# Moving four things forward in a three-phase mixture-of-experts kernel's instruction streams: the last phase's first table, the next phases' row loads, the first half's inverse roots and two scatters

## The reference, cut to what matters

```python
x = x + 0.5 * ffn(layernorm(x))      # 12 experts, each token goes to 3 of them
x = x + attn(layernorm(x))           # gates, y_t = A*y_{t-1} + u_t along 512 tokens, norm, gated product
x = x + 0.5 * ffn(layernorm(x))
# ffn: top-3 of x @ Wg (128x12), softmax weights, h = gelu(x @ Wup[e] + bup[e]) (128 -> 512),
#      y = h @ Wdown[e] + bdown[e] (512 -> 128), sum over the 3 chosen experts
```

## Time and profile before

| what | value |
|---|---|
| median of 3 runs | 632.81 us (632.74 to 634.7) |
| profiled execution | 633.43 us, its span in the trace 631.7 us |
| TensorE matmul busy | 564.4 us (89% of the span) |
| ScalarE busy | 419.8 us (66%) |
| GpSimd busy | 418.0 us (66%) |
| VectorE busy | 348.7 us (55%) |
| mean granted TensorE clock | 0.954 of full speed |

### The profile page before, as it was taken

How to read it: one execution, slowest core, us unless ns; L and a number is a source line. 1 busy time by engine, 2 the same in 40 slices (tenths; PEclk the granted TensorE clock), 3 DMA queues, 4 the chain that set the end, 5 groups by cost and what they waited for, 6 DMA issues and landing times.

```text
span 631.7 us, 17884 instructions
## 1 busy us (share of the span) xinstructions
PE 564.4 (89%) x4591; PEld 529.5 (84%) x4591; DVE 348.7 (55%) x1636; ACT 419.8 (66%) x1280; POOL 418.0 (66%) x432
## 2 busy tenths in 40 slices
PE   8469999999699999999999899999979999989505
PEld 7358999999699889879899789899979999989502
DVE  5983365371014688987727589888743532232206
ACT  2547686686366787887668688877657766656204
POOL 1137777777767775556677777066666777777774
PEclk9769999999799999999999999999999999999957
DMA  7577776789598786466478967466568888765137
GB/s 214 180 190 236 211 196 202 218 205 275 156 288 255 215 240 178 138 188 189 135 215 255 275 212 206 148 187 183 160 175 249 217 281 251 215 194 156 49 119 244
DMA packets 121847, 127.90 MB, mean 202 GB/s; under 512 B 17178, under 2 KB 84561, under 8 KB 121749
## 3 DMA queue, kind: packets, MB, share of 16 engines
q1 hardware_dynamic: 106452, 99.52, 53.2%
q0 software_dynamic: 12992, 26.11, 14.8%
q10 hardware_dynamic: 2304, 1.11, 0.6%
HBM read 96.62 MB, written 30.79 MB: 202 GB/s over the span
## 4 chain that ended last, share of the span: by engine, by line
PE 54%; DMA 13%; POOL 12%; DVE 10%; issue 8%; ACT 1%; SPq 0%; DVEq 0%; POOLq 0%; ACTq 0%
PE ps L931 20%; PE ps L944 20%; POOL YG L739 6%; DMA YG<-ys,SY 4%; POOL yk L750 3%; PE ps L799 3%; DMA xl<-xn,SG 3%; PE ps L825 2%; POOL xs L723 2%; PE ps L901 2%; DMA yk<-Ys,row 2%; DMA xs<-XN,SX 2%; PE ps L891 1%; DMA ys<-Ys 1%; DVE YG L1563 1%
## 5 line engine op out<-in xcount | busy, mean ns | idle before, releaser
L1097 ACT ACTIVATE hT<-ps,BU 128x128 f32<-128x128 f32 x944 | 269.4, 371 | 109.3 <-PE ps L931 106.7
L931 PE MATMUL ps<-xT,WU 128*128 128x128 f32 x1888 | 253.8, 278 | 4.2 <-ACT hT L1097 2.3
L944 PE MATMUL ps<-WD,hT 128*128 x1888 | 252.4, 277 | 4.8 <-DVE Ys L1635 3.7
L931 PEld LDWEIGHTS ps<-xT,WU 128*128 128x128 f32 x1888 | 233.4, 194 | 13.9 <-issue 13.9
L944 PEld LDWEIGHTS ps<-WD,hT 128*128 128x128 f32 x1888 | 231.7, 193 | 6.9 <-issue 6.8
L723 POOL DMA_INDIRECT xs<-XN,SX x144 | 144.5, 1004 | 87.6 <-issue 66.2
L739 POOL DMA_INDIRECT YG<-ys,SY x144 | 150.1, 1042 | 48.5 <-issue 40.6
L1635 DVE TENSOR_TENSOR Ys<-ps,BD 128x128 f32<-128x128 f32 x236 | 67.5, 289 | 193.4 <-PE ps L944 182.7
L708 POOL DMA_INDIRECT xl<-xn,SG x59 | 59.7, 1011 | 30.4 <-issue 14.0
L750 POOL DMA_INDIRECT yk<-Ys,row x59 | 59.0, 1000 | 18.0 <-issue 13.2
L1074 ACT ACTIVATE xT<-ps 128x512 f32<-128x512 f32 (+1 forms) x55 | 32.6, 593 | 6.6 <-PE ps L901 2.9
(11 more groups left out here) (255 smaller groups left out, 540.1 us busy)
## 6 DMA issues: line engine op xcount, KB each, us to landing
WU<-in_L_ffn_Wup_dram SPq DMA_DIRECT2D x236, 256.0 KB
ys<-Ys SPq DMA_DIRECT2D x42, 256.0 KB
xl<-xs SPq DMA_DIRECT2D x118, 66.0 KB, 3.0
xl<-xs SPq DMA_DIRECT2D x59, 64.0 KB, 1.9
WD<-in_L_ffn_Wdown_dram SPq DMA_DIRECT2D x12, 256.0 KB, 4.9
WD<-yk SPq DMA_DIRECT2D x4, 768.0 KB, 7.2
xs<-XN,SX POOLq DMA_INDIRECT x144
YG<-ys,SY POOLq DMA_INDIRECT x144
```

Source lines behind the costliest of these rows:

```text
L931: x = e.matmul(HB[i % 2][:, c * P:(c + 1) * P], WU[i % NW][:, c * P:(c + 1) * P], xT[m % 2][:, j * P:(j + 1) * P], start=True, stop=True)
L944: x = e.matmul(YB[i % 2][:, 0:D], hT[i % 3][:, c * P:(c + 1) * P], WDf[:, bass.ds(r + c * P, P)], start=(c == 0), stop=(c == C - 1))
L1097: x = e.activation(hT[i % 3][:, c * P:(c + 1) * P], HB[i % 2][:, c * P:(c + 1) * P], ACT.Gelu, bias=BU[:, bass.ds(b + c, 1)])
```

## The change

Four moves, with no arithmetic added or removed:

1. VectorE's steps A0, A1, A2 for phase 3 go from slots 51, 52, 53 to slots 49, 50, 51.
2. FETCHED is 0 for k = 0 and 1, so phase 3's scatters 0 and 1 stand ahead of all gathers. From scatter 2 on the order is as before.
3. SP's `load_rows` for the next phase's groups 0 and 1 move from behind tiles 56 and 57 to behind tiles 55 and 56, in phases 0, 1 and 2. SP's weight load of tile 56 is thereby behind the first of them, and that of tile 57 behind both.
4. In `first()`, all four `stats`, the 16 aggregations (in two groups of 8) and the root's first steps are placed between the four `chosen`. Three steps and everything else of the root's tail stay behind the one-hot arrays.

```diff
-TABLES_AT = ((34, 38), (50, 63), (51, 64))
-FETCHED = tuple(min(K * NT, 6 + (13 * k) // 25) for k in range(NTL))
+TABLES_AT = ((34, 38), (50, 63), (49, 64))
+FETCHED = tuple(min(K * NT, 6 + (13 * k) // 25) if k > 1 else 0 for k in range(NTL))
...
-                if n + 1 < NPH and k in (NTL - 3, NTL - 2):
-                    load_rows(NG * (n + 1) + k - (NTL - 3))
+                if n + 1 < NPH and k in (NTL - 4, NTL - 3):
+                    load_rows(NG * (n + 1) + k - (NTL - 4))
...
+                def spread(a, b):
+                    e.wait_ge(s_dv, dv.n)
+                    for t in range(a, b):
+                        i = e.bn_aggr(mv16[:, t, :], st16[:, t, :])
+                    dv.on(i)
+                    e.wait_ge(s_dv, dv.n)
...
-                for q in range(NQ):
-                    chosen(q)
-                    if q + 2 < NQ:
-                        stats(q + 2)
+                stats(2)
+                chosen(0)
+                stats(3)
+                spread(0, NT // 2)
+                chosen(1)
+                spread(NT // 2, NT)
+                dv.on(e.tensor_scalar(v16[:], mv16[:, :, 1], 1e-5, None, ALU.add))
+                e.wait_ge(s_dv, dv.n)
+                dv.on(e.tensor_scalar(nr16[:].bitcast(I32), v16[:].bitcast(I32), -0.5, RSQRT_SEED, ALU.mult, ALU.add))
+                e.wait_ge(s_dv, dv.n)
+                dv.on(e.tensor_tensor(na16[:], v16[:], nr16[:], ALU.mult))
+                e.wait_ge(s_dv, dv.n)
+                chosen(2)
+                dv.on(e.tensor_tensor(nb16[:], na16[:], nr16[:], ALU.mult))
+                e.wait_ge(s_dv, dv.n)
+                dv.on(e.scalar_tensor_tensor(nb16[:], nb16[:], R1, nb16[:], ALU.add, ALU.mult))
+                e.wait_ge(s_dv, dv.n)
+                dv.on(e.scalar_tensor_tensor(na16[:], nb16[:], R0, na16[:], ALU.add, ALU.mult))
+                dv.on(e.scalar_tensor_tensor(nr16[:], nb16[:], R0, nr16[:], ALU.add, ALU.mult))
+                e.wait_ge(s_dv, dv.n)
+                chosen(3)
...
-                for t in range(NT):
-                    i = e.bn_aggr(mv16[:, t, :], st16[:, t, :])
-                dv.on(i)
...
```

## The result

| | median | runs | ratio to before, 95% interval |
|---|---|---|---|
| before | 634.70 us (632.74 to 636.22) | 9 | |
| after | 628.62 us (626.4 to 631.2) | 9 | 0.9903 (0.9881 to 0.9924) |

The change is faster by 6.2 us where 6.2 us were forecast; the interval allows 4.8 to 7.5, so that the two agree to a tenth is luck. The profiled execution of after took 631.2 us (span 629.5 us) and is the slowest of its nine, against 633.43 us of before: this pair shows 2.2 us. So I read from it the steps, and the sum from the medians.

The account below looks back on a forecast made before the run. Path: VectorE to SG, POOL in phase 0, TensorE and VectorE in phases 1 and 2, POOL in phase 3. 2.98 + 1.6 + 1.58 gives 6.2 us: 627.3 from the profiled 633.43, median forecast 626.7 us, range 625.2 to 629.4.

Parts of the forecast that it names:

- Part 4, 1.58 us: Start of kernel: L1526 waits for TensorE's counts, starts near 21.03 not 22.61, so SG and POOL's stream come 1.58 us earlier.
- The upper bound of 2.5 us: Start of kernel: the most part 4 could gain, if TensorE's counts started sooner.
- Part 1, 1.6 us: End of phase 2: VectorE's K starts 1.6 us earlier, and so do POOL's last 12 scatters.
- Part 2, 2.98 us: Boundary 2/3: two scatters fill POOL's 3.28 us idle, leaving the usual 0.30, so 2.98 us gained.
- Part 3, nothing: Phase boundaries: earlier row loads gain nothing at 0/1 and 1/2, and add nothing to the sum.
- The held weight load: Boundaries: tile 56's weight load waits behind the rows, costed at nothing; as the slower rival about 635 us, chance 0.04.
- The signs that missed: Boundary 2/3: row load near 463.9, 12 scatters near 462.1, L750 rows near 477.6; POOL without a hole to about 618.5.
- Those by which a term vanishes: K not earlier or the start's gain lost: 628.3 us, chance 0.15; only the two scatters count: 630.2 us, 0.06.
- the rival by which it is more: End of phase 2: L not late or K 2.6 us earlier, 7.2 us gained, 625.6 us, chance 0.12.
- the first, third and fourth rival: K not earlier or start's gain lost, 628.3 us, 0.15; more than forecast, 625.6, 0.12; VectorE stops POOL's descriptors, 628.9, 0.03.
- the second's: Boundary 2/3: only the two scatters count, 2.6 us gained, 630.2 us, chance 0.06.
- The one by which VectorE stops POOL's descriptors: End of phase 2: A1 and A2, 2.3 us, are added to POOL's path, gain 3.9 us, 628.9 us, chance 0.03.

Follow-up runs that it names:

- roots: Only part 4 added to the kernel before: 632.46 us, ratio 0.9972.
- no_rows: The whole change without part 3, row loads left as in the kernel before: 627.04 us, ratio 0.9884.
- again: The changed kernel unaltered, run and profiled a second time: 628.01 us beside 634.07 for the kernel before, ratio 0.9893.
- fillers6: The whole change without part 3, with 6 instead of 20 fillers ahead of the counts: 628.42 us, ratio 0.9887.
- rows_b: Only part 3 added to the kernel before, repeated on another chip: 633.94 us beside 635.64, ratio 0.9973.
- rows_02_b: The whole change, but row loads moved only at boundaries 0/1 and 2/3, repeated: 628.14 us, ratio 0.9896.
- rows: Only part 3 added to the kernel before, in the slow job: 954.36 us beside 955.65, ratio 0.9967.

## Why the forecast was right, and where it was not

- **Part 4, 1.58 us.** Right: SG 1.63 us earlier, first gather 1.7 us earlier over ten profiles, 1.8 us by time (0.4 to 3.0). L1534 started at 20.97 where 21.0 was said, and SG at 36.79 where near 37.0 was said. The reason given for the bound is wrong, though: not only the fillers keep the counts from starting sooner, VectorE's own scan does too. The upper bound of 2.5 us could not have been reached by removing them. And the term was carried through phase 0 by the reading that POOL has no hole there, which is wrong: 1.31 us stand at 150.26 us before. The gain passes all the same: the stretch is 124.5 to 126.5 us with part 4 and 124.9 to 126.7 without.
- **Part 1, 1.6 us.** Right in its mechanism, a little small. From the start of the last quarter's residual add (L1312) to POOL's first scatter, the four profiles without part 1 need 13.64 to 13.67 us and the six with it 11.84 to 11.86: 1.8 us. K starts 9.99 us after L1312 (11.79 before). I had let the row maxima start 0.5 us later than before. They start 6.98 us after L1312, and 6.69 before, so 0.3. That this passes to the end by itself is argued from the chain, as part 1 alone has no usable time. VectorE before, then after, with K in the earlier trace rows before:

```profile
451.68 0.69 DVE L1312 TENSOR_TENSOR X<-X,ps 128x512 f32<-128x512 f32 x1 [1.02 <-PE ps L891]
```

```profile
453.84 0.69 DVE L1312 TENSOR_TENSOR X<-X,ps 128x512 f32<-128x512 f32 x1 [0.79 <-PE ps L891]
...
457.68 0.45 DVE L1428 TENSOR_TENSOR ge<-iotl,enda 128x288 f32<-128x288 f32 x1
...
460.03 0.16 DVE L1363 TENSOR_SCALAR eR<-RR 1x24 uint32<-1x24 f32 x1
...
463.83 0.21 DVE L1262 TENSOR_TENSOR SL<-ps,RC 128x48 f32<-128x48 f32 x1
```

- **Part 2, 2.98 us.** Right beside part 1: the fourth leg is 15.43 to 15.46 us in all six profiles that have parts 1 and 2, and 18.44 before. That this gives 2.99 is partly luck, as roots, with the same edits there as before, has 18.94.
- **Part 3, nothing.** Right for the whole change as far as the times tell, but for an incomplete reason. The text looked at boundaries 0/1 and 1/2 and found nothing to gain. That holds at 0/1: SyncE's load follows the 36th scatter by 2.68 to 2.70 us in all ten profiles. At 1/2 the load does come sooner behind the 36th scatter with the move (2.96 to 3.10 us in three profiles, 3.37 to 3.77 in the other seven), but TensorE turns the rows 5.54 to 5.55 us behind it, and 5.54 to 5.94 without. It did not ask what an earlier load does at boundary 2/3, where alone it is worth 1.9 us and closes the same hole as part 2. Terms that end in one hole do not add: the trace shows it in the fourth leg. The times lean that way, as the parts alone sum to 1.8 + 4.8 + 1.7 = 8.3 us and the whole is 6.2 and, run again, 6.8, but their intervals, over 1 us to each side, do not prove it.
- **The held weight load** cost nothing that shows: in the first tiles of phases 1 to 3 no `up` has idle time of over 0.3 us ahead of it, in any of the ten profiles.
- **The signs that missed.** SyncE's first row load of phase 3 was forecast near 463.9, POOL's 12 scatters near 462.1 and the L750 rows near 477.6. They came at 466.85, 465.69 and 481.14, 3 to 3.6 us late. Phase 0 took 1.1 us longer in this execution than in that of before, and the third leg 2.7 us longer than with part 1's gain; 2.19 + 0.63 us of that are L901's two waits for rows in phase 2. In no_rows the three signs are at 463.70, 461.66 and 477.11. POOL's stream ends at 622.5 us, where 618.5 was said, and at 617.8 in no_rows. I had also counted a transfer from the wrong scatter: 3.96 us from issue to load is 2.68 from the right one. It has no part in the sum.
- **The rivals.** Those by which a term vanishes are excluded where the term is made, by the first leg, K's chain and the fourth leg; that nothing of it is lost in the third leg rests on the times, as that leg runs from 297.8 to 302.3 us. K came 1.8 us earlier and not 2.6, so the rival by which it is more did not come as told. The chances do not add up as the text has them: the forecast, the first, third and fourth rival make 0.90, which leaves 0.01 of the second's 0.06 for faster, and not most of it. The one by which VectorE stops POOL's descriptors would lengthen scatters beside A1 and A2. In the profile after, A1 and A2 stand from 457.68 to 460.19, and POOL's scatters beside them keep their 1.29 us:

```profile
457.17 0.98 POOL L723 DMA_INDIRECT xs<-XN,SX  x1 [0.31 <-issue]
458.46 0.98 POOL L723 DMA_INDIRECT xs<-XN,SX  x1 [0.30 <-issue]
459.75 0.98 POOL L723 DMA_INDIRECT xs<-XN,SX  x1 [0.30 <-DMA xs<-XN,SX]
461.03 0.98 POOL L723 DMA_INDIRECT xs<-XN,SX  x1 [0.30 <-issue]
```

  The Trainium skill's page "SBUF — State Buffer", section "Who interferes with whom", has the rule of an exclusive port lock for VectorE's two-port modes. The same section gives `tensor_tensor` no such mode and `tensor_reduce` none on this chip, so the forecast applied it too widely: at most the five short `tensor_scalar` steps of A2 come under it, about 1 us and not 2.3. None of these scatters is late, so the trace shows no lock for them either.

**What stays open.** Whether part 3 costs something in phase 2. L901 waits near 355 us for 2.19, 1.35 and 1.17 us in the three profiles that have the row loads moved at boundary 1/2 (after, again, rows_b), and for 0.66, 0, 0, 0, 0, 1.21 and 0.45 us in the seven that do not. The third leg leans the same way: with part 1, 301.76 and 300.95 against 297.82, 299.27, 299.57 and 299.99 us; without it, 302.32 (rows_b) against 299.47, 300.89 and 301.28. But fillers6 has 1.21 us without the move, so the move is not needed for the wait. SyncE has short pauses only there, and how far it is behind at the row load of that tile changes from run to run: 33.7 us after the phase's first row load before, 33.6 in fillers6, 34.1 in again, 34.4 in rows_b and 35.5 in after, all with a wait, 32.7 in rows_02_b with its short one, and 32.5 to 32.9 in the four without any. By time, the whole change with and without part 3 differ by 1.0 us with intervals of 1.2 us and more to each side. A leaning, not a finding. The kernel that leaves the row loads where they were showed no loss against the changed one.

## What to carry to other kernels

When one engine is full in the first and the last phase, cut the run at that engine's instructions: start of its stream, holes in it, stream, tail. Here the gains of three different cuts (1.7, 1.8 and 3.0 us) sum to 6.5, near the 6.2 and 6.8 by time. Edits that close the same hole can't both be paid for it, so price a part alone and in company. Before a bound is named after the instruction that stands ahead of a wait, look for a second one that ends within a few tenths of it.

## What the runs showed of the hardware

- A single profile is uncertain by 1 to 2 us on this kernel: a stretch of identical instructions (phase 0, 59 gathers and 36 scatters) took 124.53 to 126.74 us (123.9 to 124.5 without POOL's holes), while a short chain (L1312 to the first scatter) repeats to 0.03 us.
- POOL's indirect DMAs of 128 rows came at a steady pace where nothing was waited for: 0.98 us and a pause of 0.30 for a scatter, 1.32 us each over the 107 of phase 3.
- The kernel before took 629 to 636 us on one chip (median 634.07) and 955.65 us on the same chip some minutes later; the next job, 635.64 us, ran on another chip, so whether the first one recovered is not known. In the slow job the profile of rows shows 133 GB/s of memory traffic in place of 202 and a mean granted clock of 0.81, with TensorE standing still for long pieces. A baseline in the same job is needed to see this at all.
- Where TensorE's granted clock rises in phase 0 differs between executions: from 38 to 50 us its mean was 0.73 before, 0.57 after, 0.90 in no_rows and 0.86 in fillers6. The clock has two levels, 1.2 and 2.4 GHz, and these are means over both: in the profile after, the first `up` steps took 2.05 us for eight products, near the lower level, in no_rows 1.13, at the upper. Ahead of it TensorE had done the same in both: idle for 6.2 or 6.3 us up to 27.1 or 27.2, short pieces, then 16 fillers in 3.65 us. The first `down` starts at 48.92 us in after and at 46.23 in no_rows, 2.7 us apart. Whether POOL's stream feels it is open: the three profiles with 0.89 to 0.91 have phase 0 legs of 124.5 to 125.2 us, the other seven 124.9 to 126.7. From 8 to 38 us the clock was 0.76 before and in no_rows, and 1.00 in fillers6, which has 14 fillers fewer. The fillers are not shown to be the cause: rows_02_b has all 20 and 1.00 as well.
- A wait cost TensorE more than its length. Before, it stood 2.88 us ahead of phase 3's first turn; the eight `down` products behind it took 2.07 us and the next eight `up` products 1.62, where either takes 1.06 in the profile after, without the wait. The granted clock was 0.61 from 470.6 to 475 us before, and 1.00 over the same tiles after (466 to 475 us).
